# Full attention: the fourth head's first tile one step later, peaks one maximum later, sums of two key tiles together

## The reference

```python
q = (hidden_states @ Wq.T + bq).reshape(b, t, H, HD)      # H = 16 heads of HD = 16
k = (hidden_states @ Wk.T + bk).reshape(b, t, HKV, HD)    # HKV = 4, each used by G = 4 heads
v = (hidden_states @ Wv.T + bv).reshape(b, t, HKV, HD)
...
scores = jnp.einsum('bthd,bshd->btsh', q, k) * scale
probs = jax.nn.softmax(scores, axis=2)                    # no mask: all 2048 keys
context = jnp.einsum('btsh,bshd->bthd', probs, v).reshape(b, t, DIM)
```

## Time and profile before

| what | value |
|---|---|
| median of 3 runs (lowest to highest) | 3688.42 us (3686.24 to 3691.95) |
| the profiled execution, whole | 3693.39 us |
| its span, first to last instruction | 3691.6 us |
| busy over the span: PE, DVE, ACT, POOL | 89%, 74%, 60%, 26% |
| mean granted TensorE clock | 0.949 |
| a unit of full attention (start to start) | 44.0 us written out, 44.5 us in the loop |
| two plain steps of a unit | 5.27 us |

### The profile page before, as it was taken

How to read it: one execution, slowest core, us unless ns; L and a number is a source line. 1 busy time by engine, 2 the same in 40 slices (tenths; PEclk the granted TensorE clock), 3 DMA queues, 4 the chain that set the end, 5 groups by cost and what they waited for, 6 DMA issues and landing times. The chain is left out here.

```text
span 3691.6 us, 55325 instructions
## 1 busy us (share of the span) xinstructions
PE 3270.0 (89%) x18162; PEld 1635.2 (44%) x18162; DVE 2747.2 (74%) x4130; ACT 2229.4 (60%) x3970; POOL 954.3 (26%) x906
## 2 busy tenths in 40 slices
PE   7848888997899978996679999999999999977996
PEld 3326777776566646773312222222222222214664
DVE  6639999998566654444688888888888888835665
ACT  5659999998000002221248888888888888862432
POOL 7529999996000000001300000000000000001000
PEclk9979999999899989998879999999999999998998
DMA  4447443321211136313210000000000010011001
GB/s 131 164 139 184 126 104 95 101 58 39 91 54 55 38 68 154 80 46 103 87 25 14 22 14 21 14 21 14 22 14 21 15 24 14 9 34 42 23 23 46
DMA packets 218533, 216.73 MB, mean 59 GB/s; under 512 B 63954, under 2 KB 164434, under 8 KB 217492
## 3 DMA queue, kind: packets, MB, share of 16 engines
q1 hardware_dynamic: 218276, 213.41, 20.9%
HBM read 145.99 MB, written 67.37 MB: 58 GB/s over the span
## 5 line engine op out<-in xcount | busy, mean ns | idle before, releaser
L1720 DVE TENSOR_REDUCE attn_part_max<-attn_pM 128x1 f32<-128x1024 f32 x1024 | 1204.9, 1219 | 161.7 <-PE attn_pM L1775 158.5
L1700 ACT ACTIVATE attn_probs<-attn_pE 128x512 f32<-128x512 f32 x2048 | 1089.8, 597 | 205.4 <-PE attn_pE L1824 200.9
L1824 PE MATMUL attn_pE<-attn_q,attn_k_exp 128*128 128x512 bf16 x2048 | 628.5, 385 | 31.6 <-ACT attn_q L1672 24.7
L535 POOL TENSOR_TENSOR scan_dbu<-scan_du,scan_b_all 128x2048 f32<-128x2048 f32 x128 | 578.2, 4549 | 15.0 <-DVE scan_h L594 13.2
L1795 PE MATMUL attn_pA<-attn_probs,attn_v 128*32 128x512 f32 x4096 | 560.3, 604 | 0.0
L594 DVE TENSOR_TENSOR_SCAN scan_h<-scan_abar,scan_states,scan_dbu 128x512 f32<-128x512 f32 x384 | 458.5, 1290 | 0.0
L1824 PEld LDWEIGHTS attn_pE<-attn_q,attn_k_exp 128*128 128x128 bf16 x2048 | 139.0, 97 | 608.5 <-ACT attn_probs L1700 464.7
L608 PE MATMUL scan_hT<-scan_ident,scan_h 128*128 128x128 f32 x2048 | 327.4, 284 | 68.0 <-ACT scan_hcT L546 26.0
L559 ACT ACTIVATE scan_abar<-scan_delta,scan_decay 128x512 f32<-128x512 f32 x512 | 374.7, 732 | 17.5 <-DVE scan_h L594 17.4
L546 ACT ACTIVATE scan_hcT<-scan_hT,scan_c_t 128x512 f32<-128x512 f32 x512 | 370.0, 723 | 1.2 <-PE scan_hT L608 1.1
L1653 POOL TENSOR_TENSOR attn_peak_parts<-attn_peak,attn_zero 128x4 bf16<-128x4 f32 x128 | 26.3, 205 | 1277.5 <-DVE attn_peak L1724 1277.5
(11 more groups left out here) (274 smaller groups left out, 3637.3 us busy)
## 6 DMA issues: line engine op xcount, KB each, us to landing
scan_b_all<-mid_BC SPq DMA_DIRECT2D x32, 1024.0 KB, 10.3
causal_rwB<-mid_rwT SPq DMA_DIRECT2D x64, 256.0 KB, 4.3
attn_q<-mid_q_parts SPq DMA_DIRECT2D x224, 64.0 KB, 2.4
mid_gT<-front_gT SPq DMA_DIRECT2D x8, 1024.0 KB, 7.6
mid_uT<-front_uT SPq DMA_DIRECT2D x8, 1024.0 KB, 9.2
mid_dT<-front_dT SPq DMA_DIRECT2D x8, 1024.0 KB, 4.3
scan_delta<-mid_dT SPq DMA_DIRECT2D x8, 1024.0 KB, 8.0
scan_u_in<-mid_uT SPq DMA_DIRECT2D x8, 1024.0 KB, 10.4
```

Of the source, the lines that this page charges most:

```text
L535: nc.gpsimd.tensor_tensor(dbu[:, G % NDBU, :, :], du[:, u % 2, :, :], b_row, ALU.mult).then_inc(dbu_ready, 1)
L1700: nc.scalar.activation(probs[:, kt % 4, h, :], pE[:, bank(item), :], ACT.Exp, scale=SCALE).then_inc(exp_done, 1)
L1720: nc.vector.reduce_max(part_max[:, h, j, i:i + 1], pM[:, m % 2, :], AXIS_X).then_inc(max_read, 1)
L1824: nc.tensor.matmul(pE[:, bank(item), :], k_exp[:, par, kt * 128:(kt + 1) * 128], q[:, qc, h, :], start=True, stop=True).then_inc(e_psum, 1)
```

## The change

Four things change, all in the order of work; every instruction remains, with its shape.

- e3, the fourth head's first key tile, and the row before it leave step 0. Step 0 is e0, e1, both maxima, e2. Step 1 is row, e4, e5, both maxima, e6, then the sums of tiles 14 and 15 of the last unit, then e3, e7.
- From step 3 on, the sums of two key tiles follow each other at the end of every second step: tiles 0 and 1 in step 3, 2 and 3 in step 5, up to 12 and 13 in step 15.
- DVE takes the peaks of heads 0, 1 and 2 after the first maximum of the next head instead of before it (in steps 4, 8 and 12 between that step's two maxima). The fourth stays behind the last maximum.
- Counters follow: e items are counted in their new order, and a new wait keeps the partial maxima of a head until the last unit's peak has read them.

```diff
@@ step_items
         if kt == 0:
-            return [("e", 0), ("e", 1), ("e", 2), ("row", G - 1), ("e", 3)]
+            return [("e", h) for h in range(G - 1)]
+        if kt == 1:
+            return [("row", G - 1)] + [("e", G + h) for h in range(G - 1)] + [("e", G - 1), ("e", 2 * G - 1)]
@@ UNIT
+    E_ORDER = [item[1] for item in UNIT if item[0] == "e"]
+    E_COUNT = {e: i + 1 for i, e in enumerate(E_ORDER)}
+    KT_COUNT = [max(E_COUNT[kt * G + h] for h in range(G)) for kt in range(KT)]
@@ scalar
-                                    act.wait_ge(e_psum, u * E_UNIT + item[1] + 1)
+                                    act.wait_ge(e_psum, u * E_UNIT + E_COUNT[item[1]])
@@ vector, take_max
+                    if j == 0 and i == 0:
+                        at_least(dve, peak_ready, (u - 1) * G + h + 1)
                     nc.vector.reduce_max(part_max[:, h, j, i:i + 1], pM[:, m % 2, :], AXIS_X).then_inc(max_read, 1)
-                    if m % M_HEAD == M_HEAD - 1:
-                        dve.wait_ge(max_read, u * M_UNIT + m + 1)
-                        at_least(dve, parts_ready, (u - 1) * G + h + 1)
-                        nc.vector.tensor_reduce(peak[:, h, :], part_max[:, h, :, :], AXIS_X, ALU.max, negate=True).then_inc(peak_ready, 1)
+                def take_peak(h, u):
+                    dve.wait_ge(max_read, u * M_UNIT + (h + 1) * M_HEAD)
+                    at_least(dve, parts_ready, (u - 1) * G + h + 1)
+                    nc.vector.tensor_reduce(peak[:, h, :], part_max[:, h, :, :], AXIS_X, ALU.max, negate=True).then_inc(peak_ready, 1)
@@ vector, body
                                 take_max(2 * kt, u + 1)
+                            if not end and kt and 2 * kt % M_HEAD == 0:
+                                take_peak(2 * kt // M_HEAD - 1, u + 1)
+                            if not end:
                                 take_max(2 * kt + 1, u + 1)
+                            if not end and kt == KT - 1:
+                                take_peak(G - 1, u + 1)
@@ tensor, sums
-                    pe.wait_ge(exp_done, u * E_UNIT + kt * G + G)
+                    pe.wait_ge(exp_done, u * E_UNIT + KT_COUNT[kt])
@@ tensor, body
-                            take(items[0])
-                            take(items[1])
+                            pre = 3 if kt == 1 else 2
+                            for item in items[:pre]:
+                                take(item)
                             if not end:
                                 both_maxima(kt)
-                            take(items[2])
-                            if kt == 0 and not start:
-                                sums(u - 1, KT - LAG, par if qc else 1 - par)
-                            for item in items[3:]:
+                            take(items[pre])
+                            if kt == LAG - 1 and not start:
+                                for late in range(KT - LAG, KT):
+                                    sums(u - 1, late, par if qc else 1 - par)
+                            for item in items[pre + 1:]:
                                 take(item)
-                            if kt == 1 and not start:
-                                sums(u - 1, KT - 1, par if qc else 1 - par)
                             if kt == LAG:
                                 pe.wait_ge(v_in[par], (pair + 1) * 16)
-                            if kt >= LAG:
+                            if kt > LAG and kt % 2:
+                                sums(u, kt - LAG - 1, par)
                                 sums(u, kt - LAG, par)
```

More of the change, by code:

```diff
@@ L1695, in body @@
                                 if item[0] == "e":
-                                    h = item[1] % G
-                                    act.wait_ge(e_psum, u * E_UNIT + item[1] + 1)
+                                    e_kt, h = item[1] // G, item[1] % G
+                                    act.wait_ge(e_psum, u * E_UNIT + E_COUNT[item[1]])
                                     if h == 0:
                                         at_least(act, pv_done, u * KT + kt - 3)
-                                    nc.scalar.activation(probs[:, kt % 4, h, :], pE[:, bank(item), :], ACT.Exp, scale=SCALE).then_inc(exp_done, 1)
+                                    nc.scalar.activation(probs[:, e_kt % 4, h, :], pE[:, bank(item), :], ACT.Exp, scale=SCALE).then_inc(exp_done, 1)
                                 elif item[0] == "row":
@@ L1738, in _ @@
                     take_max(m, 0)
+                    if m and m % M_HEAD == 0:
+                        take_peak(m // M_HEAD - 1, 0)
+                take_peak(G - 1, 0)
                 def body(bg, pair, par, first, last):
@@ L1763, in bank_free @@
                     if prior[0] == "e":
-                        at_least(pe, exp_done, v * E_UNIT + prior[1] + 1)
+                        at_least(pe, exp_done, v * E_UNIT + E_COUNT[prior[1]])
                     elif prior[0] == "row":
```

## The result

The changed kernel takes 3876.36 us (median of 4, 3874.61 to 3883.46) against 3690.18 us (median of 4, one run more than in the table ahead) for the kernel before: 1.0511 times as long, 95% interval 1.0498 to 1.0524, 186 us more. The forecast was 3874, +186.

A forecast was written before the change was run, and what follows sets the result against it. PE nearly full, its even order just fitting the pM ring with DVE; pairing makes PE wait. Units of 50.1 us against 44.00 (15 x 6.1) and 44.45 (16 x 5.7), plus 3 for the last unit: +186, 3874 us, range 3847 to 3915.

The forecast's parts named there:

- The ring: DVE must free a pM buffer: first maximum matmul of a step to second of the next, at least 2.85 us.
- 3.25: PE's chain without slack from an odd step's second maximum to the next even step: 3.25 us, making pairs 6.10.
- Steps 0 and 1: Start of a unit, where four e items behind two sums wait for a pE bank: 6.74 us.
- The peaks: In steps 4, 8 and 12 the peak lengthens the 2.85 us by 0.08 each, 0.24 a unit.
- the new wait: Maxima on DVE wait for the last unit's peak, over a unit earlier; claimed to cost nothing.
- its bound for the loop: If units in the loop keep their extra 0.45 us, the forecast time rises by 7 us.
- The rows: Rows 0 to 2, matmuls of 0.39 us, fit where PE waits anyway in steps without sums: a real saving.
- The last unit: Without maxima, the pE banks set 5.22 us for two steps, 0.42 more seven times: +3 us.
- PE's busy share of a unit: Sign that the forecast is right: the share of a unit in which PE is busy falls to about 88%.
- PE alone setting the pace: Rival: PE alone bounds the kernel, pairs take 4.99 us, units about 42.0, time 3620 us; chance 0.06.
- The clock: Rival: PE's idle pieces lower its clock; 3955 us if in a tenth of the pairs, over 4600 in all; chance 0.03.
- The stall of the fourth row at its new place: Rival: POOL's parts come late and PE waits at the row in step 1; +24 us, 3898; chance 0.04.

The follow-up runs named there:

- half maxima: DVE reads 512 of each maximum's 1024 columns, in both kernels: changed kernel 3755.47 us (1.0168 of the kernel before), kernel before 3671.05 us (0.9937).
- half of both: DVE reads half of each maximum's columns and ACT computes half of each tile's exponentials: changed kernel 3635.9 us, kernel before 3657.02 us.

## Why the prediction was right

**The ring.** Both of its terms held: 2.85 (2.84 in pairs without a peak) and 3.25 (3.26). The pairing alone came to 49.44 us a unit where the expectation had 49.48. That it is the ring through `pM` and not DVE's amount of work follows from three runs together: half maxima give back 3.27 us a unit in the changed order and 0.17 in the order before, and moving only e items out from behind the wait, with DVE's work untouched, gives 0.54 in a pair without a row. No run gave `pM` a third buffer, the other way to loosen this ring.

**Steps 0 and 1** were summed at 6.74 and measured 6.74; with `out` 6.54 and 6.53. The parts were there in time: 1.29 us after the peak, the row 1.70 after it, 0.4 to spare where 0.5 was worked out. What the sum missed is hidden in the changed kernel and shows only without the pairing: ACT is late in step 2, 0.37 us.

**The peaks.** Taken at 0.08 each, measured 0.06 to 0.07 in written-out units (6.17 against 6.10). The step that failed in this point is the new wait, priced at nothing because it is long true: in the loop it costs 0.09 four times a unit (6.84 for steps 0 and 1, 6.25 for the pairs with a peak), 0.36 x 16 = 6 us, which the range covered with its bound for the loop.

**The rows.** "A real saving against now" was too much said. A row costs the order before only 0.18 us (5.40 to 5.42 against 5.24, and as much with half maxima, 5.40 against 5.22, where no ring hides anything), since it runs beside the sums; its 0.39 is a duration and not what it adds. In the changed order it is indeed free: with the pairing alone, pairs with and without a row take 6.10. The sum, which took units and not rows, didn't depend on the size.

**The last unit** was summed at +3 us and measured 39.20 - 35.96 = 3.2.

**The whole.** +186 forecast and +186 measured between medians. That they agree to 1 us is luck. The profiled executions differ by 181 us: the stage grew by 187.8, and the other stages were 6.6 us shorter. Within the stage two misses met: the loop's 6 us are missing from the sum, and the stretch up to the first `move_sums` and the last one with maxima grew by 5.3 and 5.2 us instead of 6.1.

**A sign that failed.** PE's busy share of a unit was to fall from 98% to about 88%; it fell to 91%. The waits are there, but the page counts part of each as busy.

**The rivals.** PE alone setting the pace is refuted as a description of this kernel, and the runs with half of both show that even without DVE and ACT in the way a pair would cost 5.20, not 4.99: this rival was priced without the banks of `pE`. The Trainium skill's advice to run matmuls back to back in batches ("Perfetto Trace Analysis", section "Matmul Optimizations") rests there on the engine's power scaling and not on the price of a matmul. Here the batch made the second sum cheaper (0.86 instead of 1.00) and the kernel slower, with a unit's granted clock at 1.00 in both orders. The clock didn't fall in 30 of the 31 stretches from one `move_sums` to the next, though PE waits up to 0.67 us for DVE in them. The exception is the unit in which the loop turns: behind 2.60 us of PE idle the clock is 0.50 for 2 us, and the unit's mean is 0.97. The pairing isn't the cause: the kernel before with late peaks alone shows 0.90 there, after 3.26 us idle, and the kernel before itself 1.00 after 2.89. The stall of the fourth row at its new place exists, but only where steps are short, and there the ring covers it.

**What else can be gained.** Of the change's three parts, one pays by itself: row and e3 one step later, sums left apart, 0.9964 of the kernel before.

## What to carry to other kernels

Where two engines pass buffers back and forth, write down the ring: latency, the consumer's work for the buffers, and the release, and compare it with the distance between two uses in the producer's order. An even order can sit exactly on it, as here; then a batching that shortens one of the distances leaves the producer waiting. Here that cost some 0.85 us a pair of steps, to save 0.23 of PE's time at most. Before an instruction is moved to relieve an engine, look whether its new place lies inside such a ring: a peak of 0.07 us was hidden outside it (plain pairs took 5.24, and 5.22 with half the maxima's work) and paid for within (5.31).

## What the runs showed of the hardware beyond this

The f32 sum of four heads costs 1.00 us alone and 0.86 as the second one of a batch, and two in a batch take 1.86 in every run that has them. Four bf16 matmuls with 3 columns of weights (a row) right ahead of such a sum add 0.18 to its 1.00 and not a turn of their own, since three of the four heads start beside them. A reduction over 512 instead of 1024 columns of PSUM takes 686 instead of 1219 ns, an exponential of 256 instead of 512 columns 383 instead of 604. A second wait that is already true isn't free on DVE: 0.43 us from matmul to reduction became 0.50 to 0.52, depending on the order of the two waits and on whether the unit is written out or in the loop. Where the loop turns, PE stands idle for 1.9 to 3.4 us, and in 9 of the 13 kernels the granted clock of that unit is then 0.90 to 0.97.
